# A scoring pass over 128 tiles: groups of 16 instead of 8, the small operations of a group woven into the next, and buffers three deep

## What is computed

```python
x = x + 0.5 * ffn(layernorm(x))     # router picks 128 of every 1024 tokens; only these change in ffn
x = x + attention(layernorm(x))     # 8 heads of 32 within 256 numbers, low-rank q, k, v
x = x + 0.5 * ffn(layernorm(x))
```

## Time and profile before

| | us |
|---|---|
| median of three runs (4714.65 to 4730.82) | 4718.86 |
| the profiled execution | 4714.7 |
| its span in the trace | 4713.0 |
| first scoring pass (0 to 167.3) | 167.3 |
| second scoring pass (4152.7 to 4359.5) | 206.8 |

### The profile page before, as it was taken

The page is one execution under the profiler, slowest core; times in us unless marked ns, Lnnn a source line. Parts: engine busy times, 40 slices in busy tenths (PEclk is TensorE's granted clock), DMA queues, the critical chain, the costliest instruction groups (busy, mean ns, idle before and its releaser), DMA issues. The chain is left out here.

```text
span 4713.0 us, 73300 instructions
## 1 busy us (share of the span) xinstructions
PE 3747.0 (80%) x21202; PEld 1462.6 (31%) x21202; DVE 3330.6 (71%) x4776; ACT 3227.8 (68%) x6609; POOL 2553.9 (54%) x966
## 2 busy tenths in 40 slices
PE   0157588399999999999999999999999999910176
PEld 0034355133333333333333333333333333300143
DVE  8744366688777777777777777777777777468644
ACT  4143266288888888888888887888888888823043
POOL 0011000177677777776777777677777777743111
PEclk9988788699999999999999999999999999955588
DMA  6300399677887887887787788788788787776100
GB/s 217 115 10 5 112 345 356 157 158 154 168 172 165 173 168 163 171 175 157 157 174 168 166 169 170 154 169 177 158 176 172 160 175 150 147 221 228 63 5 5
DMA packets 326039, 743.24 MB, mean 158 GB/s; under 512 B 26060, under 2 KB 209888, under 8 KB 270112
## 3 DMA queue, kind: packets, MB, share of 16 engines
q0 software_dynamic: 57216, 407.92, 43.5%
q1 hardware_dynamic: 234880, 297.04, 21.2%
q10 hardware_dynamic: 33568, 33.69, 2.1%
HBM read 198.90 MB, written 136.48 MB: 71 GB/s over the span
## 5 line engine op out<-in xcount | busy, mean ns | idle before, releaser
L1613 ACT ACTIVATE at_probs<-at_ps_s 128x512 f32<-128x512 f32 x4096 | 2256.2, 613 | 349.3 <-PE at_ps_s L1734 270.6
L1498 DVE TENSOR_REDUCE at_part_max<-at_ps_max 128x3 f32<-128x1536 f32 x1024 | 1801.1, 1759 | 480.1 <-PE at_ps_max L1647 472.4
L1476 POOL TENSOR_TENSOR at_pool_sum<-at_pool_sum,at_probs 128x2048 f32<-128x2048 f32 x384 | 1771.8, 4614 | 618.9 <-DMA at_probs<-at_probs 617.5
L1734 PE MATMUL at_ps_s<-at_qs,at_ks 97*128 97x512 f32 (+1 forms) x4096 | 1536.1, 453 | 39.7 <-ACT at_probs L1613 18.5
L1681 PE MATMUL at_ps_acc<-at_probs,at_v 128*32 128x512 f32 x8192 | 1101.4, 610 | 0.9 <-ACT at_probs L1613 0.9
L1734 PEld LDWEIGHTS at_ps_s<-at_qs,at_ks 97*128 97x128 f32 (+1 forms) x4096 | 631.3, 189 | 1153.0 <-ACT at_probs L1613 820.6
L1500 DVE TENSOR_REDUCE at_part_max<-at_max_copy 128x1 f32<-128x512 f32 x1024 | 692.0, 676 | 0.0
L1562 ACT COPY at_max_copy<-at_ps_max 128x512 f32<-128x512 f32 x1024 | 609.9, 596 | 91.2 <-PE at_ps_max L1647 90.9
L1647 PE MATMUL at_ps_max<-at_ks,at_qs 32*128 32x512 f32 x4096 | 527.1, 502 | 71.1 <-DMA at_ks<-qk_parts 37.4
L1453 POOL DMA_DIRECT2D at_probs<-at_probs x384 | 346.6, 903 | 230.4 <-PE at_ps_acc L1681 222.6
L1647 PEld LDWEIGHTS at_ps_max<-at_ks,at_qs 32*128 32x128 f32 x4096 | 198.6, 184 | 430.0 <-issue 363.4
(11 more groups left out here) (195 smaller groups left out, 2772.5 us busy)
## 6 DMA issues: line engine op xcount, KB each, us to landing
at_probs<-at_probs POOLq DMA_DIRECT2D x384, 1024.0 KB, 8.3
qk_parts<-pr_hi SPq DMA_DIRECT2D x32, 1024.0 KB, 6.2
qk_parts<-pr_lo SPq DMA_DIRECT2D x32, 1024.0 KB, 6.1
at_qs<-qk_parts SPq DMA_DIRECT2D x320, 64.0 KB, 4.9
at_ks<-qk_parts SPq DMA_DIRECT2D x80, 256.0 KB, 7.1
s_x<-in_x SPq DMA_DIRECT2D x16, 1024.0 KB, 7.8
after_ffn<-s_y ACTq DMA_DIRECT2D x16, 1024.0 KB, 8.6
pr_x<-after_ffn SPq DMA_DIRECT2D x8, 2048.0 KB, 12.0
```

The costliest lines, as they stand in the source:

```text
L1476: nc.gpsimd.tensor_tensor(acc, a, probs[:, c % RING], ALU.add).then_inc(pool_added, 1)
L1498: nc.vector.reduce_max(part_max[:, 0:HG - 1, t, c], ps_max[:, 0:HG - 1], AX.X).then_inc(three_max_done, 1)
L1613: nc.scalar.activation(probs[:, c % RING, h], ps_s[:, BANK[j]], ACT.Exp, scale=SCALE).then_inc(exp_done, 1)
L1734: nc.tensor.matmul(ps_s[:, BANK[j]], ks[rows, g, h, c * P:(c + 1) * P], qs[rows, un % NQB, h, :], start=True, stop=True).then_inc(scores, 1)
```

## The change

Groups are of 16 tiles (`TG = T`), so there are 8, one a sequence, and each buffer exists three times. `sall` and the small columns keep their meaning, with 16 numbers each. All loops over groups are written out; no `Fori` is left in the pass.

- Loads go out in halves of 8 tiles, each with its own semaphore, both halves of a group behind the same wait. The router weights come behind the first half of group 0.
- VectorE's 17 small operations are numbered by `affine_step(b, n)`. Those of group b - 1 stand in group b: number 2t behind the statistics of tile t, number 2t + 1 behind its product, so that they fill tiles 0 to 8. Each still waits for what it reads. Those of the last group stand alone at its end.
- ScalarE computes y in halves of 8 tiles with a store of 1 MiB after each. A buffer's loads wait for both halves (`y_half_done`).
- GpSimd waits for the half that a quad of tiles lies in.

```diff
-    TG = T // 2
-    GROUPS = B * T // TG
-    NBUF = 4
+    TG = T
+    GROUPS = B
+    NBUF = 3
     ROWS = TG * P
+    HALF = TG // 2
...
+            def load(b, half):
+                k = b % NBUF
+                rows = slice(b * ROWS + half * HALF * P, b * ROWS + (half + 1) * HALF * P)
+                tiles = slice(half * HALF, (half + 1) * HALF)
+                sp.dma_start(xb[:, k, tiles], x[rows, :].rearrange("(t p) d -> p t d", p=P)).then_inc(x_in[2 * k + half], 16)
+                if adding:
+                    sp.dma_start(ab[:, k, tiles], add[rows, :].rearrange("(t p) d -> p t d", p=P)
+                                 ).then_inc(a_in[2 * k + half], 16)
+
+            load(0, 0)
             sp.dma_start(w[:], w_router.partition_broadcast(P)).then_inc(w_in, 16)
...
+            load(0, 1)
+            for b in range(1, GROUPS):
+                if b >= NBUF:
+
+                    sp.wait_ge(products_done, (b - NBUF + 1) * TG)
+                    sp.wait_ge(y_half_done, (b - NBUF + 1) * 2)
+                load(b, 0)
+                load(b, 1)
...
+                elif n == 6:
+                    dve.wait_ge(std_ready, b + 1)
+                    nc.vector.reciprocal(v[7], v[6]).then_inc(dve_own, 1)
+                elif n == 7:
+                    dve.wait_ge(dve_own, own + 6)
+                    nc.vector.tensor_tensor(v[8], v[7], v[7], ALU.mult).then_inc(dve_own, 1)
...
+            for b in range(GROUPS):
+                k = b % NBUF
+                for t in range(TG):
+                    if adding and t % 4 == 0:
+                        dve.wait_ge(added, b * (TG // 4) + t // 4 + 1)
+                    elif not adding and t % HALF == 0:
+                        dve.wait_ge(x_in[2 * k + t // HALF], b // NBUF * 16 + 16)
+                    nc.vector.bn_stats(stats[:, k, t, :], xb[:, k, t, :]).then_inc(stats_done, 1)
+                    if b > 0:
+                        affine_step(b - 1, 2 * t)
+                    if b > 0 or t >= 4:
+
+                        dve.wait_ge(products_done, b * TG + t - 3)
+                    nc.vector.tensor_tensor_reduce(out=junk[:, t % 4, :], in0=pw[:, 0:D], in1=xb[:, k, t, :],
+                                                   scale=1.0, scalar=0.0, op0=ALU.mult, op1=ALU.add,
+                                                   accum_out=sm[:, k, 11, t:t + 1]).then_inc(products_done, 1)
+                    if b > 0:
+                        affine_step(b - 1, 2 * t + 1)
+            for n in range(17):
+                affine_step(GROUPS - 1, n)
...
+            for b in range(GROUPS):
+                k = b % NBUF
+                act.wait_ge(var_ready, b + 1)
+                nc.scalar.activation(sm[:, k, 6, :], sm[:, k, 5, :], ACT.Sqrt).then_inc(std_ready, 1)
+                act.wait_ge(affine_ready, b + 1)
+                if b >= NBUF:
+
+                    act.wait_ge(y_out[k], b // NBUF * 32)
+                for half in range(2):
+                    for t in range(half * HALF, half * HALF + HALF):
                         last = nc.scalar.activation(yb[:, k, t, :], xb[:, k, t, :], ACT.Identity,
                                                     scale=sm[:, k, 0, t:t + 1], bias=sm[:, k, 1, t:t + 1])
...
+                    last.then_inc(y_half_done, 1)
+                    act.wait_ge(y_half_done, 2 * b + half + 1)
+                    rows = slice(b * ROWS + half * HALF * P, b * ROWS + (half + 1) * HALF * P)
+                    act.dma_start(y[rows, :].rearrange("(t p) d -> p t d", p=P),
+                                  yb[:, k, half * HALF:half * HALF + HALF]).then_inc(y_out[k], 16)
```

More of the change, by code:

```diff
@@ L102, in score_pass @@
         w_copied = sem("w_copied")
-        x_in = [sem(f"x_in{i}") for i in range(NBUF)]
-        a_in = [sem(f"a_in{i}") for i in range(NBUF)]
+        x_in = [sem(f"x_in{i}") for i in range(2 * NBUF)]
+        a_in = [sem(f"a_in{i}") for i in range(2 * NBUF)]
         added = sem("added")
@@ L149, in _ @@
             if adding:
[L150 to L157, removed]
+                for b in range(GROUPS):
+                    k = b % NBUF
+                    for q in range(TG // 4):
+                        half = q // (HALF // 4)
+                        pool.wait_ge(x_in[2 * k + half], b // NBUF * 16 + 16)
+                        pool.wait_ge(a_in[2 * k + half], b // NBUF * 16 + 16)
+                        t4 = slice(4 * q, 4 * q + 4)
+                        nc.gpsimd.tensor_tensor(xb[:, k, t4], xb[:, k, t4], ab[:, k, t4], ALU.add).then_inc(added, 1)
         @block.vector
@@ L161, in _ @@
             dve.wait_ge(w_in, 16)
[L162 to L163 removed]
+            nc.vector.reduce_sum(wsum[:], w[:], AX.X).then_inc(dve_own, 1)
             dve.wait_ge(w_copied, 1)
[L165 to L169, removed]
[L170 to L206 removed]
@@ L231, in _ @@
             for k in range(NBUF):
-                act.wait_ge(y_out[k], 16 * GROUPS // NBUF)
+                act.wait_ge(y_out[k], 32 * len(range(k, GROUPS, NBUF)))
         @block.tensor
```

103 lines of the change are left out of this document (47 added, 56 removed).

## The result

The changed kernel takes 4636.9 us (median of four runs, 4629.4 to 4643.6) against 4721.9 us (four runs, 4714.7 to 4730.8): ratio 0.9826, 95% interval 0.9804 to 0.9848. By the ratio that is 82 us or 1.7% less, by the medians 85.0 us. Forecast were 74 us.

What follows compares the result with a forecast made beforehand. VectorE was taken to bound the first pass; after the change the ScalarE loop would set it, and DMA the second's later groups. Minus 38 and minus 36 give 74 us off 4718.9: 4645 us, range 4622 to 4670.

Steps and rivals of the forecast that it cites:

- What can move: Whole program: only the two scoring passes, 167.3 and 206.8 us, can move; other stages moving over 3 us would show error.
- Price of a woven operation: VectorE, small operations between half tiles: 0.10 us each, between 0.09 and 0.205, making a group 12.4 us.
- Rival C: Woven small operations still cost 0.205 us each on VectorE, a group takes 14.2 us; 4657 us, chance 0.10.
- The loop between ScalarE and VectorE: First pass: ScalarE's y delays the next group's root, which VectorE awaits; 12.9 us a group, above VectorE's own 12.4.
- -38: First scoring pass: forecast change in us, with the last store at 123.7 where it was 161.63.
- First pass, tail: End of first pass: last chain alone to 114.7, last store at 123.7, then 5.8 us to the next stage.
- Second pass: Second scoring pass: adds hold the early weave, then DMA moves a group in 17.2 us; minus 36, about 171 us.
- The two bounds "so close": Second pass, later groups: DMA at 17.2 us, VectorE's 12.4 plus three or four stalls of 1.2 to 1.9 just below.
- rival D: Slower: three-buffer cycle of fill, score, scale, write, forecast 51 us, a third 17, would need 87; about 4725, chance 0.02.
- Rival A: Second pass: all 32 GpSimd adds hold VectorE about 1.9 us each, pass 193 us, 14 saved; 4667 us, chance 0.12.
- Rival B: Second pass: weaving cheap, lock rarely met, DMA alone bounds, near 157 us, 50 saved; 4631 us, chance 0.14.
- E: Whole kernel: no change within 0.3%, which needs 60 us to be lost in the two passes; chance 0.01.

Runs made afterwards that it cites:

- e2: Weave alone: changed kernel put back to groups of 8 tiles, four buffers and whole 1 MiB loads; first pass 146.1 us, second 201.2 us.
- e7: Changed kernel with two buffers instead of three, weave kept; first pass 186.0 us, second 268.7 us.
- e6: Changed kernel with whole loads and stores of 16 tiles (2 MiB) instead of halves; first pass 136.6 us, second 207.4 us.
- e3: Changed kernel with GpSimd's 32 second-pass additions replaced by one-column fills, all loads kept; first pass 125.0 us, second 153.3 us.
- e4: Changed kernel with GpSimd adding one tile at a time instead of four; first pass 125.1 us, second 154.5 us.
- e1: Changed kernel with the weave undone, each group's 17 small operations chained behind its own products; first pass 137.3 us, second 166.6 us.
- e9: Changed kernel with two buffers instead of three and a chain instead of the weave; first pass 142.9 us, second 206.7 us.

## Why the prediction was right

- **What can move.** The code outside the two passes is the same, and the forecast put its change at 0. Measured were -5.4 us, more than the 3 us that the prediction itself had named as a sign of being wrong. That limit was too narrow: over the runs of this study the same stages scatter by 23 us (4333.6 to 4356.6).
- **Price of a woven operation**, taken as 0.10 between 0.09 and 0.205: measured 0.085. Rival C fell with it.
- **The loop between ScalarE and VectorE**: the mechanism was right (e2 shows it alone, 7.9 us for 8 tiles), its size 12.9 was too large, 12.48 measured. The two halves of y with their issues took 9.07 of the 9.3, and root, steps and signals 3.41 of the 3.6. In the first, the gap of 0.25 in front of each store, read from the earlier trace rows, measured 0.03; second issues of 0.46 gave some of that back. That the gap was register work of the loop is inferred from the two orders of instructions and was not tested apart. Over seven groups the pass is 3.3 us shorter by it; with the first statistic at 8.05, not 8.9, and a tail 0.4 shorter, that makes the 4.3 us between -38 and -42.3, but for rounding.
- **First pass, tail.** Forecast 19.5 us from the last product to the next stage, measured about 19 (105.9 to 125.0).
- **Second pass.** The chain of group 0 held to some 16 us (15.6 measured), release of the fourth load 49 us into the pass (4151.78, which is 48.9), group 2 ended 62.5 us in by forecast and 63.2 by trace, group 3 at 82 and 81. Then 17.2 a group forecast, 17.3 measured (4183.98 to 4235.76). The pass ended 1.8 us below the forecast. The forecast let DMA set the middle and VectorE lie just below; in the trace VectorE has no room either (69.90 us of 70).
- **The two bounds "so close"** were three, all near 17. That the third, the release cycle, runs over two groups and not three I did not see: rival D's cycle of 51 us over three buffers was the wrong sum, though it gave the same 17. Its verdict stands by luck of the size; with two buffers (e7) or whole loads (e6) the same sum misled.
- **Rival A** (each add holds VectorE): 22 operations were held by 32 adds, not 32. **Rival C** was priced at 4657, 12 us from the forecast; its words "half of what it says" don't follow from that, since 62 of the 74 us would have been left. **Rival B** (lock rarely met) describes e3 and e4, 153.3 and 154.5, near its 157. **E** didn't come.
- The Trainium skill's rule on the shared port (SBUF — State Buffer, Who interferes with whom) agrees with every held row, and e3 prices it: 15.7 us. Before the change nearly as many operations were held, since chains met the lock too (35.4 us), but there they cost the pass their full length, by the sums below. The Trainium skill's figure of about 358 GB/s (DMA: Bandwidth & Descriptors, Specifications) does not bound a mix of reads and writes here: 366 over four groups, 377 in e3.

What each part was worth, as far as the runs separate it. In the first pass groups of 16 in halves gave 30.0 us and the weave on top 12.3; in the other order the weave alone gave 21.2 (e2) and the groups on top 21.1, so the parts don't simply add. In the second pass groups of 16 in halves with three buffers gave 40.1 (e1), and the weave nothing. The third buffer is part of that: with two, groups of 16 in halves give the second pass nothing (e9, 206.7) and the first 24.4. Groups of 16 with the weave and three buffers but without halves give the second pass nothing either (e6, 207.4). Groups of 16 in halves with four buffers were not tried, nor was the written-out loop by itself.

A sum tells what the second pass is made of: the length of the first pass, plus the held time, plus how much later the first statistic comes after the start of the second.

| kernel | first pass | held | later start | sum | second pass |
|---|---|---|---|---|---|
| before | 167.3 | 35.4 | 4.2 | 206.9 | 206.7 |
| e1 | 137.3 | 24.7 | 3.2 | 165.2 | 166.6 |
| e2 | 146.1 | 51.5 | 3.1 | 200.7 | 201.2 |
| changed | 125.0 | 38.3 | 3.0 | 166.3 | 169.0 |
| e4 | 125.1 | 16.2 | 2.3 | 143.6 | 154.5 |
| e3 | 125.0 | 0 | 2.3 | 127.3 | 153.3 |

In the first four the sum gives the pass within 3 us, so the held time lies on the path in full, as far as a sum can tell. By it the lock cost some 35 us before the change (no run without adds was made there), and e1's gain is fewer chains (30.0) and less held time (10.7). In e3 and e4 the sum falls far below the pass, where loads and stores keep it at 153 to 155 us. The changed kernel stands only some 15 us above that, and so the lock costs it 15.7 and not 38.

## What to carry to other kernels

A woven chain takes its cost off the busy engine but ties group b's output to group b + 1's data: count a ring of n buffers as n - 1, and ask whether the landing still fits. When several engines and the DMA are within a few per cent of one another, an experiment that eases one shows only what the ends and the fill were worth; look there first. Where two engines exclude each other by whole instructions, shorten the instructions of the one with time to spare.

## What the runs showed of the hardware

- A small operation on VectorE that does not wait for its neighbour costs 0.085 us between two large ones (0.07 to 0.10 for most), against 0.205 us in a chain.
- A held operation ends some 0.03 to 0.04 us after the add that it met, though GpSimd's next add follows at once and isn't held up by it (adds stay at 2.34 us): 2.34 us adds let one small operation by per 2.34 us, 0.72 us adds one per 0.72 us. Held time fell from 38.3 to 16.2 us though GpSimd worked 18 us longer.
- ScalarE's issue of a store after the last y tile started 0.03 us behind it in written-out code and 0.25 in the loop.
- Reads alone moved 345 GB/s in the first 32 us of the second pass, reads with writes 366 over 70 us of the changed kernel and 377 over 70 us of e3.
